# Nine reorderings in the first group's front of a fused decoder layer

## The reference

```python
# 1 attention without softmax, 16 heads of 16
q = (q @ fq1.T + bq1) * (q @ fq2.T + bq2)      # k likewise
o = (causal sum over m of (q . k_m) v_m)
x = ln(x + (o * rsqrt(mean(o*o) + eps) * norm_w) @ wo.T)
# 2 long convolution gated by a context, 8 x 8 products per head
kv = v[:, :, :, None] * ctx[:, :, None]
y = causal_conv(kv, k) + kv * skip
x = ln(x + einsum('bhijl,bhil->bhjl', y, ctx))
# 3 FFN, 4-bit weights with block scales, 2048 wide
x = ln(x + (gelu_tanh(x @ Wg.T) * (x @ Wu.T)) @ Wd.T)
```

## Time and profile before

| what | value |
|---|---|
| median of 3 runs | 545.06 us (544.81, 545.06, 546.42) |
| profiled execution, own time | 546.63 us |
| its span in the profile | 544.9 us |
| TensorE busy | 525.6 us (96%) |
| VectorE busy | 369.7 us (68%) |
| ScalarE busy | 151.1 us (28%) |
| GpSimd busy | 125.2 us (23%) |
| share of the chain that ended last | PE 83%, DVE 8%, issue 4%, DMA 2% |
| mean granted clock of TensorE | 0.991 |

### The profile page before, as it was taken

The page is one execution under the profiler, slowest core; times in us unless marked ns, Lnnn a source line. Parts: engine busy times, 40 slices in busy tenths (PEclk is TensorE's granted clock), DMA queues, the critical chain, the costliest instruction groups (busy, mean ns, idle before and its releaser), DMA issues.

```text
span 544.9 us, 8781 instructions
## 1 busy us (share of the span) xinstructions
PE 525.6 (96%) x3335; PEld 426.7 (78%) x3335; DVE 369.7 (68%) x776; ACT 151.1 (28%) x269; POOL 125.2 (23%) x196
## 2 busy tenths in 40 slices
PE   8899989899999999999999999999999999999994
PEld 8645767566888888866888888776888888888883
DVE  4898889967767668875455668876454777753335
ACT  4545210232333111242232112231333101333231
POOL 3110079210004444120003444120004571010001
PEclk9999899989999999999999999999999999999999
DMA  4563222221201210032001110031001110010001
GB/s 139 164 190 89 87 60 69 79 68 36 72 1 39 60 40 19 1 123 73 1 1 39 51 48 21 0 97 61 1 1 49 55 53 1 1 39 1 1 0 39
DMA packets 25257, 26.81 MB, mean 49 GB/s; under 512 B 2816, under 2 KB 22784, under 8 KB 25216
## 3 DMA queue, kind: packets, MB, share of 16 engines
q1 hardware_dynamic: 14752, 16.26, 9.8%
q10 hardware_dynamic: 10032, 8.43, 5.3%
q0 software_dynamic: 432, 1.57, 0.8%
HBM read 24.15 MB, written 2.10 MB: 48 GB/s over the span
## 4 chain that ended last, share of the span: by engine, by line
PE 83%; DVE 8%; issue 4%; DMA 2%; POOL 1%; ACT 1%; SPq 0%; POOLq 0%; DVEq 0%; ACTq 0%
PE bank L1135 17%; PE bank L1136 16%; PE bank L1137 16%; PE front_bank L1292 5%; PE front_bank L1295 5%; PE front_bank L1293 5%; PE front_bank L1205 3%; PE front_bank L1192 3%; PE front_bank L1135 2%; PE front_bank L1136 2%; PE front_bank L1137 2%; PE front_bank L1264 2%; PE front_bank L1237 1%; DMA xT_sb<-in_xT 1%; DMA raw_s<-in_gate_s 1%
## 5 line engine op out<-in xcount | busy, mean ns | idle before, releaser
L1135 PE MATMUL bank<-x2T_lo,ffn_hi 128*128 128x512 f32 x256 | 110.0, 430 | 1.4 <-DVE x2T_lo L1020 1.4
L1136 PE MATMUL bank<-x2T_hi,ffn_lo 128*128 128x512 f32 x256 | 101.2, 395 | 0.0
L1137 PE MATMUL bank<-x2T_hi,ffn_hi 128*128 128x512 f32 x256 | 101.1, 395 | 0.0
L1077 DVE TENSOR_TENSOR inter<-bank,inter 128x512 f32<-128x512 f32 x63 | 43.5, 690 | 82.8 <-PE bank L1137 82.5
L521 POOL TENSOR_TENSOR qbd<-qT_sb,ctxT_sb 128x256 f32<-128x256 f32 x128 | 79.4, 643 | 67.0 <-PE front_bank L1295 54.0
L471 POOL TENSOR_TENSOR ve<-ve,minus_half 128x2 f32<-128x2 f32 x24 | 17.1, 728 | 286.4 <-DVE ve L856 228.0
L711 ACT ACTIVATE inter_hi<-inter 128x512 fp32r<-128x512 f32 x63 | 39.8, 632 | 144.1 <-DVE inter L1077 144.1
L1135 PE MATMUL bank<-ffn_lo,inter_hi 128*128 128x256 f32 x256 | 76.3, 298 | 1.0 <-DVE inter_lo L1066 0.7
L698 ACT ACTIVATE inter<-bank 128x512 f32<-128x512 f32 x64 | 38.2, 598 | 130.7 <-PE bank L1137 130.7
L1136 PE MATMUL bank<-ffn_hi,inter_lo 128*128 128x256 f32 x256 | 71.5, 279 | 0.0
L1137 PE MATMUL bank<-ffn_hi,inter_hi 128*128 128x256 f32 x256 | 71.0, 277 | 0.0
(11 more groups left out here) (139 smaller groups left out, 780.8 us busy)
## 6 DMA issues: line engine op xcount, KB each, us to landing
toep_sb<-in_toep ACTq DMA_DIRECT2D x64, 128.0 KB, 2.0
xT_sb<-in_xT SPq DMA_DIRECT2D x4, 512.0 KB, 4.8
ctxT_sb<-in_ctxT SPq DMA_DIRECT2D x4, 512.0 KB, 4.6
x_sb<-in_x SPq DMA_DIRECT2D x4, 512.0 KB, 5.9
ctx_sb<-in_ctx SPq DMA_DIRECT2D x4, 512.0 KB, 6.9
out<-ctxT_sb POOLq DMA_DIRECT2D x3, 512.0 KB, 3.4
raw_w<-in_gate_p SPq DMA_DIRECT2D x8, 128.0 KB
raw_s<-in_gate_s SPq DMA_DIRECT2D x8, 128.0 KB
```

The costliest lines, as they stand in the source:

```text
L1077: nc.vector.tensor_tensor(inter[:, n % 2, :], up_ps[:, :], inter[:, n % 2, :], ALU.mult).then_inc(inter_ready, 1)
L1135: nc.tensor.matmul(ps, w_hi, x_lo, start=start, stop=False, skip_group_check=True)
L1136: nc.tensor.matmul(ps, w_lo, x_hi, start=False, stop=False, skip_group_check=True)
L1137: return nc.tensor.matmul(ps, w_hi, x_hi, start=False, stop=stop, skip_group_check=True)
```

## The change

Nine edits, all but the statistics in group 0 only:

- SyncE fetches unit 0 before it waits for `xT`.
- Every spread of group 0 is made by ScalarE.
- Group 0's values go to banks of their own (`psum[7]` and `psum[6]`); TensorE makes the second half after the scores of step 0, and these no longer wait for the values.
- The low part in score step u is that of unit 3+u instead of 4+u (`low_on_pe` covers units 3 to 10 instead of 4 to 11, so the remainder of unit 3 goes to TensorE and that of unit 11 to VectorE). The `keep_busy` product stands after both identity products instead of between them.
- ScalarE rounds group 1's tokens in score step 6 instead of after the squares.
- `stats` finishes the variances of each pair of sequences with that pair, in all groups and layer norms but the very last.
- The first skip product on TensorE stands ahead of the last convolution step, and its gate ahead of the last `conv_sum`. They use `fb[2]` and `fb[0]`.
- The two skip sums of group 0 go from VectorE (`add_skip`) to GpSimd (`skip_add`), directly onto `x_sb`; `add_conv` waits for them.
- Projections 4 and 5 of group 1 wait for the second gate and the last `conv_sum`, which free their banks, and `conv_back` for the first gate.

```diff
@@ -186,6 +186,7 @@
         end_inter, end_hi, end_lo = sems("end_inter", "end_hi", "end_lo")
+        (skip_added,) = sems("skip_added")
         rstd_ready = sems("rstd_ready1", "rstd_ready2", "rstd_ready3")
@@ -263,7 +264,7 @@
         def low_on_pe(q):
-            return FIRST_SCORE <= q + 1 < FIRST_SCORE + NU_S
+            return FIRST_SCORE <= q + 2 < FIRST_SCORE + NU_S
         def low_parts(eng, k):
@@ -291,7 +292,9 @@
         def skip_bank(g, j):
-            return fb[j] if is_last(g) or g == 0 else skip_ps[j]
+            if g == 0:
+                return fb[2 - 2 * j]
+            return fb[j] if is_last(g) else skip_ps[j]
         def ahead(g):
@@ -305,7 +308,7 @@
         def v_bank(g, j):
-            return fb[j] if ahead(g) else fb[2 + j]
+            return psum[7 - j] if g == 0 else fb[j] if ahead(g) else fb[2 + j]
         def schedule(eng, turn, front, gate, up, down, unpack, finish):
@@ -408,8 +411,8 @@
+            fetch(0)
             sp.wait_ge(ld_xT, 16)
-            fetch(0)
             fetch(1)
@@ -481,7 +484,7 @@
             def score(g, u):
-                if u + 2 < NU_S and u % 2:
+                if u + 2 < NU_S and u % 2 and g:
                     spread(g, u + 2)
             def norm(g, _):
@@ -505,6 +508,15 @@
                     skip_products(g, h // 2 + 2 - CH // 2)
+                if g == 0 and h == CH - 1:
+                    skip_add(g, 0)
+            def skip_add(g, j):
+                count(pool, sk_ready, 2, g, j + 1)
+                both = x_sb[:, 2 * j:2 * j + 2].rearrange("p b f -> p (b f)")
+                nc.gpsimd.tensor_tensor(both, both, ctx_sb[:, 2 * j:2 * j + 2].rearrange("p b f -> p (b f)"), ALU.add)\
+                    .then_inc(skip_added, 1)
             def products(g, h):
@@ -521,12 +533,15 @@
             def turn(done, prev, g, beside=nothing):
+                if prev == 0:
+                    skip_add(prev, 1)
                 if prev is not None and not is_last(prev):
...
                         beside(pair)
-                    spread(g, 1)
+                    if g:
+                        spread(g, 1)
                 if done is not None:
@@ -574,11 +589,13 @@
                         .then_inc(whi_ready, 1)
-                    if low_on_pe(n):
-                        act.wait_ge(wlo_mm, n + 2 - FIRST_SCORE)
-                        nc.scalar.activation(ffn_lo[:, m, :, c * QC:(c + 1) * QC],
-                                             low_ps[n % 2][:, :].rearrange("p (w n) -> p w n", w=2), ACT.Copy)\
-                            .then_inc(wlo_act, 1)
+                q = step - 2
+                if low_on_pe(q):
+                    m, c = units[q]
+                    act.wait_ge(wlo_mm, q + 3 - FIRST_SCORE)
+                    nc.scalar.activation(ffn_lo[:, m, :, c * QC:(c + 1) * QC],
+                                         low_ps[q % 2][:, :].rearrange("p (w n) -> p w n", w=2), ACT.Copy)\
+                        .then_inc(wlo_act, 1)
             def proj(g, p):
@@ -605,19 +622,16 @@
                                                 ACT.Copy, scale=half_sel[:, k:k + 1])
-                last.then_inc(spread_ready[0], 1)
+                last.then_inc(spread_ready[u % 2], 1)
             def score(g, u):
-                if u + 2 < NU_S and u % 2 == 0:
+                if u + 2 < NU_S and (u % 2 == 0 or g == 0):
                     spread(g, u + 2)
+                if u == NU_S - 2 and ahead(g + 1):
+                    split_x(g + 1)
             def squares(g, mt):
-                spread_done_and_square(g, mt)
-                if mt == KT - 1 and ahead(g + 1):
-                    split_x(g + 1)
-            def spread_done_and_square(g, mt):
                 count(act, o_mm, NU_S, g, NU_S)
@@ -769,7 +785,7 @@
                         if low_on_pe(q):
-                            dve.wait_ge(wlo_mm, q + 2 - FIRST_SCORE)
+                            dve.wait_ge(wlo_mm, q + 3 - FIRST_SCORE)
                         else:
@@ -843,21 +859,15 @@
-                for b in (2 * j, 2 * j + 1):
-                    if b == 2:
-                        count(dve, st_ready[ln], NB, g, 2)
+                pair = (2 * j, 2 * j + 1)
+                for b in pair:
                     nc.vector.bn_stats(st[:, ln, b, :], tile[:, b, :]).then_inc(st_ready[ln], 1)
-                if j == 0:
-                    return
-                for b in (0, 1):
+                count(dve, st_ready[ln], NB, g, 2 * j + 2)
+                for b in pair:
                     nc.vector.bn_aggr(mv[:, ln, b, :], st[:, ln, b, :]).then_inc(mv_ready[ln], 1)
-                count(dve, st_ready[ln], NB, g, 4)
-                count(dve, mv_ready[ln], NB, g, 2)
-                nc.vector.tensor_scalar(ve[:, ln, 0:2], mv[:, ln, 0:2, 1], LN_EPS, None, ALU.add).then_inc(ve_ready[ln], 1)
-                for b in (2, 3):
-                    nc.vector.bn_aggr(mv[:, ln, b, :], st[:, ln, b, :]).then_inc(mv_ready[ln], 1)
-                count(dve, mv_ready[ln], NB, g, NB)
-                nc.vector.tensor_scalar(ve[:, ln, 2:4], mv[:, ln, 2:4, 1], LN_EPS, None, ALU.add).then_inc(ve_ready[ln], 1)
+                count(dve, mv_ready[ln], NB, g, 2 * j + 2)
+                nc.vector.tensor_scalar(ve[:, ln, pair[0]:pair[1] + 1], mv[:, ln, pair[0]:pair[1] + 1, 1], LN_EPS, None,
+                                        ALU.add).then_inc(ve_ready[ln], 1)
             def normalise(g, ln, tile, into):
@@ -881,6 +891,8 @@
                     conv_sum(g, h - 1)
+                if g == 0 and h == CH - 1:
+                    gated_skip(g, 0)
             def conv_sum(g, h):
@@ -911,11 +923,15 @@
             def add_conv(g, j):
                 count(dve, cT_mm, 2, g, j + 1)
+                if g == 0:
+                    dve.wait_ge(skip_added, j + 1)
                 nc.vector.tensor_tensor(pair_of(x_sb, j), fb[2 + j][:, :], pair_of(x_sb, j), ALU.add)\
...
             def add_skip(g, j):
+                if g == 0:
+                    return
                 count(dve, half_ready, 2, g, j + 1)
@@ -926,10 +942,17 @@
+            def rest_ready(g, k):
+                if g == 0:
+                    dve.wait_ge(half_ready, k)
+                else:
+                    count(dve, y_ready[1], 2, g - 1, k)
             def x2_rest(g, j):
                 add_skip(g, j)
-                count(dve, y_ready[1], 2, g, j + 1)
+                rest_ready(g, j + 1)
                 stats(g, 1, x_sb, j)
             def join(g, k):
@@ -947,7 +970,7 @@
                 else:
-                    count(dve, y_ready[1], 2, g, 2)
+                    rest_ready(g, 2)
                     stats(g, 1, x_sb, 1)
             def norm2(g, _):
@@ -1023,7 +1046,6 @@
             def second_turn(prev, g):
                 conv_sum(prev, CH - 1)
-                gated_skip(prev, 0)
                 gated_skip(prev, 1)
@@ -1141,7 +1163,7 @@
                     if p in (4, 5):
-                        pe.wait_ge(sk_ready, 2 * (g - 1) + p - 3)
+                        pe.wait_ge(*((sk_ready, 2) if p == 4 else (z_ready, CH)))
                     elif p > 5:
@@ -1198,7 +1220,8 @@
                         count(pe, qk_ready, 4, g, 4)
-                        count(pe, v_ready, 2, g, 2)
+                        if g:
+                            count(pe, v_ready, 2, g, 2)
                     count(pe, spread_ready[u % 2], NU_S // 2, g, u // 2 + 1)
@@ -1206,8 +1229,12 @@
                     last.then_inc(s_mm, 1)
+                    if g == 0 and u == 0:
+                        vproj(g, 1)
+                        pe.wait_ge(v_ready, 1)
                 if g == 0 and u < NU_S:
-                    low_part(FIRST_SCORE + u - 1)
+                    low_part(FIRST_SCORE + u - 2)
+                    keep_busy(g, 1)
                 else:
@@ -1216,14 +1243,13 @@
                 pe.wait_ge(deq_ready, q + 1)
-                if q == FIRST_SCORE - 1:
+                if q == FIRST_SCORE - 2:
                     pe.wait_ge(minus_ready, 1)
-                if q >= FIRST_SCORE + 1:
-                    pe.wait_ge(wlo_act, q - FIRST_SCORE)
+                if q >= FIRST_SCORE:
+                    pe.wait_ge(wlo_act, q + 1 - FIRST_SCORE)
                 bank = low_ps[q % 2][:, :]
...
                                  start=True, stop=False, skip_group_check=True)
-                keep_busy(0, 1)
                 pe.wait_ge(whi_ready, q + 1)
@@ -1287,6 +1313,8 @@
                 n = NB * CI * CI
+                if g == 0 and h == CH - 1:
+                    skip(g, 0)
                 diag, off = toep_sb[:, h % NTOEP, 0:P], toep_sb[:, h % NTOEP, P:2 * P]
@@ -1297,15 +1325,25 @@
             def skips(g):
                 for j in range(2):
+                    if g == 0 and j == 0:
+                        continue
+                    skip(g, j)
+            def skip(g, j):
                     count(pe, prod_ready, 2, g, j + 1)
-                    if is_last(g) or ahead(g + 1):
```

(7 more changed lines are left out.)

## The result

| kernel | median | lowest to highest | profiled execution, its span | clock |
|---|---|---|---|---|
| before | 545.18 us (6 runs) | 543.71 to 546.42 | 546.63, 544.9 | 0.991 |
| after | 540.9 us (6 runs) | 540.4 to 542.42 | 540.84, 539.0 | 0.996 |

The ratio is 0.9916, with a 95% interval of 0.9902 to 0.993: faster. It is estimated over the single runs and is not the quotient of the medians; as a time the interval is 3.8 to 5.3 us, and the medians differ by 4.3. The forecast was 540.4.

What follows compares the result with a forecast made beforehand. TensorE bounds the kernel from 180 us on; in group 0's front, the first 108 us, three stretches answer VectorE. Gains 3.1 + 0.6 + 1.0 = 4.7 us, taken from the median 545.06, give 540.4; range 538.8 to 542.4.

Steps and rivals of the forecast that it cites:

- the rival with a chance of 0.12: Around the first gate product: one 1.2 GHz stretch of TensorE vanishes, worth 1.6 us, giving 538.8; chance 0.12.
- Early tokens: Projection start: fetching right behind `xT` removes VectorE's 1.00 us wait for the first scales; gain 1.0 us.
- The bound of 1.6 for a later `xT`: Kernel start: the early fetch could delay `xT`, losing at most 1.6 us net of slack; as rival 542.0, chance 0.05.
- Spreads: Projections: without GpSimd spreads, VectorE's mask of codes and dequantisation lose 0.6 us less; 0.3 of it kept.
- Scores ahead of half the values: Score start: score 0 waits for no values and gains 3.2 us, to 23.3; mask 0 at 24.8, mask 1 at 28.4.
- Identity products: Score stage: a step later, no weight wait; mask steps 2.80, mask 7 at 45.2 against 47.99, gaining 2.8 us.
- my first rival: Score loop stays bound: TensorE's loop near 3.0, or unit 7's data holds VectorE; 541.2 to 542.0, chance 0.16.
- Carried to the factor product: From scores through rms steps to the factor product: gain carried 3.1 us, bounds 2.4 and 3.3.
- Tokens, hidden: Before the factor product: ScalarE rounds group 1's tokens in score 6, so VectorE's subtraction no longer waits for it.
- Statistics by pairs: First layer norm: one GpSimd power, 0.75, less 0.15 for earlier aggregation; gain 0.6 us, later groups 0.
- Turn: Skip sums leave VectorE: 1.4 less 0.3 gives 1.1 at the statistics, held to 1.0 us by TensorE's projections.
- One half-clock stretch: TensorE's 1.2 GHz stretch after its wait before 107.90: one such stretch less is worth 1.6 us; chance 0.12.

Runs made afterwards that it cites:

- u1: The changed kernel with the first fetch again behind the wait for `xT`; median 542.98 us.
- u2: The changed kernel with the odd spreads of group 0 on GpSimd again; median 541.94 us.
- u3: The changed kernel with both halves of the values ahead of score 0, in their old banks; median 542.22 us.
- n2: The changed kernel with unit 3's low part before the values' second half, outputs 0 awaiting only the first, no step 0 fill-in, `x`/context loads four units later; 541.76 us.
- n1: The changed kernel with unit 11's remainder made by TensorE in score step 8 instead of by VectorE; median 539.94 us.
- u4: The changed kernel with identity products back at their old step (units 4 to 11, fill-in product between them); median 542.62 us.
- u7: The changed kernel with group 1's tokens rounded after the squares again; median 541.59 us.
- u5: The changed kernel with `stats` as before, both pairs finished together in all groups; median 541.75 us.
- u6: The changed kernel with the two skip sums of group 0 on VectorE again; median 544.01 us.
- u8: The changed kernel with the first skip product and its gate back behind the last convolution step; median 542.67 us.
- n4: The changed kernel with unit 11's remainder on TensorE, low part reordered, `x`/context loads later, and five readerless products before the first convolution product; 542.8 us.

## Why the prediction was right

The median, 540.9 for 540.4, and the stages where time was won came out as forecast. The size of the sum did not quite: the edits are worth about 3.8 us by the landmarks and about 3 by runs at equal clock, not 4.7, and a half-clock stretch that is rarer in after's runs made up for it. That second part was in the rival with a chance of 0.12, not in the sum, so the closeness of 540.4 is partly luck. By its own steps:

**Early tokens, 1.0.** u1: 1.08. The bound of 1.6 for a later `xT` did not come.

**Spreads, 0.3 of 0.6.** u2: 0.24 at mask 0, 0.13 at mask 7.

**Scores ahead of half the values, score 0 at 23.3, mask 0 at 24.8, mask 1 at 28.4.** Seen at 23.06, 24.39 and 28.00, with a zero 0.37 sooner. The places were right. As a term by itself it is small, 0.4 (u3): half of what mask 0 gained is given back before mask 1, as the three marks already said (3.6 between the masks, 3.28 before), and more at unit 7.

**Identity products, mask steps 2.80 to mask 7 at 45.2.** Mask 7 stood at 45.25, but by a wrong sum. From mask 0 to mask 7 I expected 20.4 us and after took 20.86. The steps are 2.80 and TensorE's loop is 2.74, inside my 2.6 to 3.0, except where VectorE waits 0.38 for unit 7's scales: that step is 3.27, and accounts for the missing 0.47. It is the second half of my first rival (data for unit 7 behind `x` and context), at 0.5 us and not 0.8 to 1.6. The start 0.37 sooner covered it. VectorE also stood idle 0.54 before the first dequantisation of the score stage, where the forecast had no stall. The weight buffer is not to blame: with the buffer free long before, u3 and n2 show the same 0.52. It cost little, because mask 1 waited for TensorE anyway (0.30 more), and in the steady loop no such wait is seen.

**Carried to the factor product, 3.1.** 3.18 between the profiles, but about 0.8 of it is the 1.2 GHz stretch at 54 to 58 us that before had and after has not. The edits carried 2.4, the forecast's lower bound. The one more `ffn_lo` on VectorE was said to be just hidden, "0.74 - 0.69"; it is not. n1 shows 0.47 of it in the path, and 7.48 against 6.97 from the mean squares to the factor product shows 0.5. The 0.74 us of cover in the earlier trace rows was the stretch's doing: at full clock, with the same work on VectorE, u4 has no idle time there. The forecast read it as a property of the order and had not looked at the clock of that stage. The other miss is the 0.5 lost at unit 7.

**Tokens, hidden.** u7: 0 to 0.1.

**Statistics by pairs, 0.6.** 0.52 between before and after, 0.61 by u5.

**Turn, 1.0.** 0.91. The single terms hold as well: 1.4 for two sums (u6: 1.48), 0.1 for transposes (0.15), and the wait for a skip sum gone only with the moved gate (u8: 0.60).

**One half-clock stretch, 1.6.** The mechanism is there, the price is mis-sized, and its place varies. With the earlier trace rows gone the rest of the kernel took 0.89 less, and 429.24 before is the only one of all the profiles above 428.5. 1.6 counted TensorE's lost work; beside it, lie in a time in which TensorE also waits for masks and tokens, so part of the lost time was slack. Over the profiles the price is 0.3 to 0.4 at 50 to 54 us, where VectorE is last anyway, 0.8 at 54 to 58 in before, where it has less work, 0.9 at 108 to 113, and 1.1 to 1.4 at 68 to 74. Taking the difference from the median was right in direction: the profiled execution of before lay 1.5 above its median, that of after on it. But the median was not free of stretches either: 28 of 31 runs of before had at least one by their clock, one of six of after.

## What to carry to other kernels

When a stage has two engines that are nearly equally late, undo each edit by itself and count from a common zero inside the kernel: here the medians mixed the parts with the clock, and the landmarks could separate them. Look at the granted clock of a stage before taking idle time in it for cover: 0.74 us on VectorE was there only because TensorE ran a stretch at half clock. Compare single runs at equal clock as well as medians. And a move to the slower engine pays when that engine idles and its input can be made sooner; the second half of that is an edit of its own.

## What the runs showed of the hardware

TensorE's stretches at 1.2 GHz, each some 3 to 4 us long, came in three places: 50 to 58 us (before, u2, u3, u7), 68 to 74 (u1, u5, u6), 108 to 113 (before only). Before had two, the others named one, and seven of the fourteen profiles none. The last two follow waits of TensorE of 1.48 and 1.39 us, which all kernels have (but n4, with 0.33 for the first), so the wait alone doesn't decide. What does was not found.

Behind two loads of 512 KB each, the scales of a fetch of 256 KB were there for VectorE only 7.1 and 7.5 us after their issue. In the score stages of all profiles VectorE's only waits for data were for a unit fetched behind these loads, 0.26 to 1.37 us.

The start of the kernel, up to the first remainder of the tokens, varied between 8.00 and 9.20 us from profile to profile. It is noise of the size of most parts of this change.
